# The last 290 columns of the first layer's score tiles computed by GpSimd instead of VectorE

## The reference, cut to what matters

```python
e = jax.nn.leaky_relu(a1[src] + a2[dst], negative_slope=0.2)
m = jax.ops.segment_max(e, dst, num_segments=n)
w = jnp.exp(e - m[dst])
denom = jax.ops.segment_sum(w, dst, num_segments=n)
agg = jax.ops.segment_sum((w / denom[dst])[:, :, None] * ft[src], dst, num_segments=n)
```

## Time and profile before

| | us |
|---|---|
| median of 3 runs | 1221.65 |
| lowest, highest | 1218.46, 1225.67 |
| the profiled execution | 1217.92 |
| its span, first to last instruction | 1216.2 |
| DVE busy | 1014.4 (83%) |
| PE busy | 1087.6 (89%) |
| ACT busy | 645.7 (53%) |
| POOL busy | 164.7 (14%) |

### The profile page before, as it was taken

How to read it: one execution, slowest core, us unless ns; L and a number is a source line. 1 busy time by engine, 2 the same in 40 slices (tenths; PEclk the granted TensorE clock), 3 DMA queues, 4 the chain that set the end, 5 groups by cost and what they waited for, 6 DMA issues and landing times.

```text
span 1216.2 us, 20805 instructions
## 1 busy us (share of the span) xinstructions
PE 1087.6 (89%) x7873; PEld 910.4 (75%) x7873; DVE 1014.4 (83%) x1729; ACT 645.7 (53%) x1069; POOL 164.7 (14%) x155
## 2 busy tenths in 40 slices
PE   2888668998898889699999999999979999999996
PEld 1444446666666666499999999999878888788885
DVE  7789799999999999887686599999987766277864
ACT  0544689999899999622301256676721321222431
POOL 4000000000000000000019021111510006231111
PEclk9999969999999999899999999999989999999998
DMA  3011401020202020453233711203042123235111
GB/s 137 1 65 53 142 1 55 31 85 2 85 1 85 1 91 2 164 177 123 79 116 134 245 39 43 78 1 112 28 155 71 40 66 139 103 122 205 66 63 49
DMA packets 39858, 98.94 MB, mean 81 GB/s; under 512 B 4467, under 2 KB 17147, under 8 KB 39765
## 3 DMA queue, kind: packets, MB, share of 16 engines
q1 hardware_dynamic: 39766, 97.66, 23.5%
HBM read 70.74 MB, written 26.90 MB: 80 GB/s over the span
## 4 chain that ended last, share of the span: by engine, by line
PE 43%; DVE 38%; issue 14%; ACT 2%; DVEq 1%; DMA 1%; POOL 1%; SPq 0%; POOLq 0%; ACTq 0%
PE psum L985 13%; PE psum L902 12%; DVE R L1501 12%; PE psum L1013 9%; DVE R L1487 7%; DVE R L1638 5%; DVE R L1648 5%; PE psum L693 3%; DVE et_lo L1665 1%; PE psum L966 1%; PE psum L795 1%; DMA x_spill<-R 1%; PE psum L996 1%; DVE R L1371 1%; PE psum L950 1%
## 5 line engine op out<-in xcount | busy, mean ns | idle before, releaser
L844 PE MATMUL psum<-ident,R 128*128 128x128 f32 (+3 forms) x1200 | 160.9, 283 | 44.9 <-ACT R L1126 44.7
L844 PEld LDWEIGHTS psum<-ident,R 128*128 128x128 f32 (+3 forms) x1200 | 130.6, 144 | 86.7 <-ACT R L1126 74.2
L1501 DVE CUSTOM_DVE_ANT_0 R<-R,LC 128x1250 f32<-128x1250 f32 x120 | 175.0, 1459 | 3.8 <-ACT LC L1100 3.8
L1126 ACT ACTIVATE R<-R,row_max 128x1250 f32<-128x1250 f32 x120 | 161.5, 1345 | 5.2 <-DVE row_max L1501 4.0
L858 PE MATMUL psum<-R 128*64 128x256 f32 (+3 forms) x1200 | 149.6, 389 | 0.0
L1142 ACT COPY R<-psum 128x1280 f32<-128x1280 f32 x120 | 143.3, 1194 | 1.5 <-PE psum L844 1.5
L902 PE MATMUL psum<-w_hi,x1T_hi 128*128 128x256 f32 (+1 forms) x480 | 136.4, 284 | 2.4 <-issue 1.6
L902 PE MATMUL psum<-w_lo,x1T_hi 128*128 128x256 f32 (+1 forms) x480 | 135.3, 282 | 0.0
L902 PE MATMUL psum<-w_hi,x1T_lo 128*128 128x256 f32 (+1 forms) x480 | 135.1, 281 | 0.0
L1943 POOL TENSOR_TENSOR rstd<-rstd,minus_half 128x1 f32<-128x1 f32 (+1 forms) x40 | 32.0, 800 | 721.8 <-DVE rstd L1514 721.8
L1487 DVE SCALAR_TENSOR_TENSOR R<-R 128x1250 f32<-128x1250 f32 x80 | 121.8, 1522 | 0.0
(11 more groups left out here) (220 smaller groups left out, 2599.0 us busy)
## 6 DMA issues: line engine op xcount, KB each, us to landing
R<-rows_spill SPq DMA_DIRECT2D x20, 625.0 KB, 5.2
rowbuf<-rows_spill SPq DMA_DIRECT2D x14, 625.0 KB, 5.3
lc_spill<-LC SPq DMA_DIRECT2D x9, 625.0 KB
LC<-lc_spill SPq DMA_DIRECT2D x9, 625.0 KB, 5.8
res_spill<-colbuf SPq DMA_DIRECT2D x36, 128.0 KB, 2.2
R<-res_spill SPq DMA_DIRECT2D x9, 512.0 KB, 3.6
R<-in_x_dram SPq DMA_DIRECT2D x1, 3456.0 KB
res_spill<-R SPq DMA_DIRECT2D x9, 384.0 KB
```

What stands on the lines that cost most here:

```text
L844: last = e.transpose(turn0[r % 2][0:m, s, 0:n_dst], ring[0:n_dst, r % RING0, s * P:s * P + m], ident[0:n_dst, 0:n_dst])
L1126: e.activation(ring[0:m, r % RING0, :], ring[0:m, r % RING0, :], ACT.Exp, bias=row_max[0:m, r % RING:r % RING + 1], scale=-1.0, accum_out= ...
L1501: e.tensor_tensor_reduce(slot, slot, LC[0:m, i, :], 1.0, MIN_CEILING, ALU.add, ALU.min, row_max[0:m, r % RING:r % RING + 1]).then_inc(S.le ...
```

## The change

- DVE's `leaky0` covers columns 0 to 959 instead of all 1250, still in one instruction, with the operators turned round: a minimum of `row` with the scalar, and then the addition of `row_slope`.
- POOL gets a loop over all 120 row tiles. For each it takes the minimum of the last 290 columns with the scalar (TENSOR_SCALAR, one SBUF tensor as input), waits for its own result, and adds `row_slope` (TENSOR_TENSOR, two SBUF tensors). It waits for the same row loads and the same `turned0` as DVE does.
- `least0` waits for both parts, and SP waits for both before it loads over a row buffer.
- The stored rows are scaled by 0.2 and 0.8 (negated) instead of 0.2 and 1, on ACT, with as many instructions.

```diff
-                for part, factor in ((0, -SLOPE), (1, -1.0)):
+                for part, factor in ((0, -SLOPE), (1, SLOPE - 1.0)):
...
-                e.scalar_tensor_tensor(out=ring[0:m, r % RING0, :], in0=row_slope[0:m, :],
-                                       scalar=att_part0[0:m, i, H0 + h:H0 + h + 1], in1=row[0:m, :], op0=ALU.add,
-                                       op1=ALU.min).then_inc(S.leaky0, 1)
+                here = slice(0, POOL_AT0)
+                e.scalar_tensor_tensor(out=ring[0:m, r % RING0, here], in0=row[0:m, here],
+                                       scalar=att_part0[0:m, i, H0 + h:H0 + h + 1], in1=row_slope[0:m, here],
+                                       op0=ALU.min, op1=ALU.add).then_inc(S.leaky0, 1)
...
                 e.wait_ge(S.leaky0, r + 1)
+                e.wait_ge(S.leaky0_pool, r + 1)
...
+            e.wait_ge(S.terms0, 1)
+            for r in range(ROWS0):
+                n, j = divmod(r, 4)
+                h, i = rows0(n)[j]
+                m = rows[i]
+                row_slope, row = row_bufs0[h % SETS0]
+                here = slice(POOL_AT0, N)
+                if n % U == 0 and j in (0, 2):
+                    e.wait_ge(S.row_in[h % SETS0], 2 * 16 * (h // SETS0 + 1))
+                if r >= RING0:
+                    e.wait_ge(S.turned0, r - RING0 + 1)
+                e.tensor_scalar(ring[0:m, r % RING0, here], row[0:m, here], att_part0[0:m, i, H0 + h:H0 + h + 1], None,
+                                ALU.min).then_inc(S.pool_part0, 1)
+                e.wait_ge(S.pool_part0, r + 1)
+                e.tensor_tensor(ring[0:m, r % RING0, here], ring[0:m, r % RING0, here], row_slope[0:m, here],
+                                ALU.add).then_inc(S.leaky0_pool, 1)
```

More of the change, by code:

```diff
@@ L341, in gnn_kernel @@
         S.row_in = [sem(f"row_in_{b}") for b in range(SETS0)]
+        S.leaky0_pool, S.pool_part0 = sem("leaky0_pool"), sem("pool_part0")
         S.leaky0, S.least0, S.exp0, S.turned0, S.kept0, S.used0, S.agg0, S.agg_turned, S.agg_kept = (
@@ L396, in gnn_kernel @@
         TURNS = 2 * NT - 1
+        POOL_AT0 = 960
         def side_bank(use):
@@ L536, in sync_program @@
                 e.wait_ge(S.leaky0, 4 * (U * (past // 2 + 1) - 1) + 2 * (past % 2) + 2)
+                e.wait_ge(S.leaky0_pool, 4 * (U * (past // 2 + 1) - 1) + 2 * (past % 2) + 2)
                 load_row0(h)
             e.wait_ge(S.leaky0, 4 * U * (G0 - 1))
+            e.wait_ge(S.leaky0_pool, 4 * U * (G0 - 1))
             e.wait_ge(S.res_out, 16 * NT)
@@ L543, in sync_program @@
             e.wait_ge(S.leaky0, ROWS0)
+            e.wait_ge(S.leaky0_pool, ROWS0)
             load_w1(2)
```

## The result

The changed kernel takes 1284.4 us (median of 4 runs, 1281.94 to 1286.84) against 1221.1 us of the kernel before on the same chips: a ratio of 1.052, with a 95% interval of 1.0497 to 1.0545. The forecast was 1278 us, in a range of 1245 to 1318.

A forecast was written before the change was run, and what follows sets the result against it. DVE was taken as the bound at 2.81 us a row tile; +0.54 for the addition, +0.25 for the minimum and -0.30 saved give +0.49, over 116 tiles +57 us: 1221.65 + 57 = 1278 us, range 1245 to 1318.

The forecast's parts named there:

- DVE is the bound, and ACT the next.: First-layer stage: DVE's two instructions set 2.81 us a row tile; ACT's 2.70 leaves at most 0.11 to win.
- the faster rival: First-layer stage: no turns, DVE comes down to 2.51 us, ACT's 2.70 ends last; 1210 us, chance 6%.
- The saving of 0.30 us: DVE's `leaky0`: 290 of 1250 columns fewer save 0.30 us a row tile.
- The addition's delay of 0.54 us: POOL's two-input addition of 290 columns makes the next DVE instruction stand still for 0.54 us a row tile.
- The lock on whole records: Rival: DVE stands still for POOL's whole records, 0.81 us for the addition; 1341 us in all, chance 4%.
- The minimum's delay of 0.25 us: POOL's minimum of 290 columns delays DVE by 0.25 us a row tile, from an assumed record of 0.52 us.
- POOL has two turns in a row tile, DVE two instructions: they fall into step.: First-layer row tiles: one POOL turn at each DVE boundary, with POOL's results still in time.
- Nothing of DVE's wait on `leaky0_pool` is then seen.: At `least0`: POOL's part is ready in time, so DVE shows no wait for it.
- DVE idle and POOL the bound: Sign in the profile after: DVE idle and released by POOL would mean POOL is the bound and the minimum mis-sized.
- `least0` at 1.7 to 2.0 us as the test: Profile after: `least0`, unchanged in shape, would take 1.7 to 2.0 us instead of 1.46 if turns delay DVE.
- PE's clock: PE, busy 2.61 of 3.30 us, might fall to half clock; ten us so would lose 4 us.
- T: Experiments' theory: reading POOL instructions take exclusive turns against DVE's two-input ones; the minimum takes two, so three turns meet two boundaries.

The follow-up runs named there:

- with DVE undisturbed: Two kernels against the change: POOL fills the ring slots once and nobody computes the 290 columns, 1211.6 us; both POOL instructions replaced by fills, 1210.5 us.
- the addition alone: Against the change, POOL's minimum is left out and POOL only adds row and `row_slope` in the 290 columns: 1245.7 us.

## Why the prediction held, and which of its steps didn't

- **DVE is the bound, and ACT the next.** Right: with DVE undisturbed the kernel takes 1211.6 and 1210.5 us, where the faster rival had 1210.
- **The saving of 0.30 us** in `leaky0`: right, 1.52 to 1.22 us.
- **The addition's delay of 0.54 us**, from the delays behind 256 and 768 columns: right, 0.50 and 0.61 in turn in the first part of the stage, 0.53 in the second, 0.42 to 0.53 with the addition alone. The lock on whole records, 0.81, was rightly set aside. The page of the Trainium skill (SBUF — State Buffer, SBUF: two separate sides) is right in kind, since one reads and the other stands, and its "for the whole instruction" isn't borne out: 0.53 stands beside a lone record of 0.80.
- **The minimum's delay of 0.25 us:** right in size, 0.23 in the first part and 0.15 and 0.21 in the second, but luckily so, for its reasoning wasn't. I took the lone record for 0.52 us and the delay for the record less 0.27. The record is 1.00 us (and 1.73 at 580 columns, 2.5 ns a column), and the delay is much less than that.
- **"POOL has two turns in a row tile, DVE two instructions: they fall into step."** This held for the first 28 tiles behind the masks, for the reason given: 2.51 us, 0.55 for the addition (the mean of 0.50 and 0.61) and 0.23 for the minimum are 3.29, measured 3.30. For the 82 behind them it is the step that failed: the minimum with its scalar in SBUF loses a boundary, and DVE waits for POOL. Two tiles of 6.70 us are 5.02 of undisturbed DVE work, delays of 0.54, 0.15 and 0.21, a wait of 0.69, and 0.09 by which two DVE records no longer overlap because of it. That is 0.45 us of delays a tile and 0.39 of waiting, 0.84 rather than the 0.79 predicted. Here the forecast was near by luck: too much delay and no wait nearly cancelled. Over the stage these 82 tiles cost 44.8 us more than before, where 0.49 each makes 40.2; the 28 cost 13.4 (forecast 13.7), and the rest, at the masks and at the end, 4.8 (forecast 2.9). Most of the forecast's miss of 6 us lies in the waits.
- **"Nothing of DVE's wait on `leaky0_pool` is then seen."** Right in the first part, wrong in the second for the same reason. The prediction named the sign of it, DVE idle and POOL the bound, but gave it no chance of its own and put it down to a mis-sized minimum. The record was mis-sized; yet with a constant, nearly as long, POOL keeps up save at the tiles of 98 rows.
- **`least0` at 1.7 to 2.0 us as the test:** right in the first part, 1.95 and 2.06; half right in the second, 1.67 in the tiles of the short minimum and 1.45 in the others.
- **PE's clock** fell now and then (0.90 to 1.00 in the windows behind 200 us) and cost nothing that the chain shows.

T's "two turns, one for the scalar" is shown as far as that in the second part of the stage an SBUF scalar makes the minimum miss a boundary, that a constant there doesn't save beside tiles of 98 rows, and that a third boundary in each tile cures it. T isn't the whole account: in the first part the same minimum, scalar and all, needs one boundary. There the addition stands ahead of `least0`, later ahead of `leaky0`; it may be that the scalar is read in the same stop of DVE as the addition, but nothing here tests that. That the first of the turns is really the read of the scalar, and short, isn't seen in any record either.

No version here beats the kernel before with the whole computation done. The best that leaves work out of the 290 columns gains 0.8%, and POOL has no way to do that work without reading.

## What to carry to other kernels

Before work goes from DVE to an idle POOL, look at what DVE reads at that time: behind back-to-back instructions with two SBUF inputs, each POOL instruction that reads stops DVE once (here some 0.53 us for the addition of 290 columns and 0.2 for their minimum, where the two together saved DVE 0.30). Count POOL's turns against DVE's boundaries as well as its microseconds, and take a per-partition scalar from SBUF for a possible turn more: here every second minimum lost a boundary in 82 row tiles, and none in the 28 ahead of them. And read the next engine's floor first: here ACT at 2.70 of 2.81 us left less than 1% to win.

## What the runs showed of the hardware that was not expected

- With a per-partition scalar from SBUF, POOL's minimum lost a boundary in the second part of the stage (records of 3.20 and 1.00 us in turn), where one with a constant took 1.84 us each time save at tiles of 98 rows. In the first part it lost none (2.21 us).
- The same instructions, in the same order on each engine, ran in two patterns within one execution: 3.30 us a row tile up to 277 us, 3.36 behind.
- The minimum of 290 columns takes 1.00 us alone, but stops DVE for 0.15 to 0.23 only; the addition takes 0.80 alone and stops it for 0.42 to 0.61.
- Fills by POOL, 0.34 us each, run beside DVE's two-input instructions without any delay of either.
